# Gating expert rows in their slot and adding them to a DRAM copy of x

## The reference, cut to what matters

```python
# x: (8, 256, 256) float32 = 2048 tokens of 256 numbers = 8 images of 256 x 256
h = layernorm(x); h = instance_norm(h over the tokens of an image) * gamma[id] + beta[id]
gates, idx = top_k(softmax(h @ router_w), 2); gates /= gates.sum(-1)     # 2 of 8 experts per token
hid  = relu(einsum('nd,edf->nef', h, exp_w1) + exp_b1)                   # 256 -> 1024
eout = einsum('nef,efd->ned', hid, exp_w2) + exp_b2                      # 1024 -> 256
f = x + sum over the token's 2 experts of gate * eout                    # the field
df = -(d/dx (A0 f) + d/dy (A1 f)) + 0.5 * (d2/dx2 (B0 f) + d2/dy2 (B1 f) + 2 mixed terms of B2 f)
out = maximum(f + df * dt[image], 0)
```

## Time and profile before

| | us |
|---|---|
| median of 3 runs (lowest to highest) | 358.14 (357.94 to 358.56) |
| the profiled execution: its own time | 359.56 |
| its span, first to last instruction | 357.7 |

### The profile page before, as it was taken

The page is one execution under the profiler, slowest core; times in us unless marked ns, Lnnn a source line. Parts: engine busy times, 40 slices in busy tenths (PEclk is TensorE's granted clock), DMA queues, the critical chain, the costliest instruction groups (busy, mean ns, idle before and its releaser), DMA issues.

```text
span 357.7 us, 6562 instructions
## 1 busy us (share of the span) xinstructions
PE 304.5 (85%) x1963; PEld 265.1 (74%) x1963; DVE 285.9 (80%) x523; ACT 252.5 (71%) x465; POOL 161.1 (45%) x135
## 2 busy tenths in 40 slices
PE   1759231999999999999999999999999988477896
PEld 0648231999999999999999999999999978132334
DVE  3896683678889889988988989988898893299991
ACT  1688214696998799699699979969988870188421
POOL 2565306333345545533533554453354413287650
PEclk9999755799999999999999999999999999699999
DMA  8903453976687877766768786776784500596822
GB/s 271 379 4 112 125 196 119 381 250 217 202 263 265 287 251 236 270 225 223 281 217 275 264 278 205 239 256 220 226 274 158 158 3 30 160 309 118 179 100 79
DMA packets 49860, 74.27 MB, mean 208 GB/s; under 512 B 3349, under 2 KB 40751, under 8 KB 49712
## 3 DMA queue, kind: packets, MB, share of 16 engines
q1 hardware_dynamic: 45104, 62.29, 53.4%
q0 software_dynamic: 4368, 11.54, 10.5%
q10 hardware_dynamic: 368, 0.20, 0.2%
HBM read 63.51 MB, written 9.31 MB: 204 GB/s over the span
## 4 chain that ended last, share of the span: by engine, by line
PE 71%; DVE 12%; DMA 8%; ACT 3%; issue 3%; POOL 1%; SPq 1%; DVEq 0%; POOLq 0%; ACTq 0%
PE psum L1005 23%; PE psum L1032 19%; PE psum L1034 10%; PE psum L998 5%; PE psum L974 2%; PE psum L1000 2%; DMA raw_b<-in_L_cond_exp_w_dram 2%; PE psum L1027 2%; DMA t_y<-y_rows 1%; PE psum L1069 1%; PE psum L913 1%; PE psum L924 1%; DMA x_sb<-t_y 1%; DMA gathered<-h_rows,src_cur 1%; DMA x_sb<-in_x_dram 1%
## 5 line engine op out<-in xcount | busy, mean ns | idle before, releaser
L798 POOL DMA_INDIRECT gathered<-h_rows,src_cur x40 | 65.4, 1635 | 123.3 <-DVE src_cur L1336 95.6
L1032 PE MATMUL psum<-w_split,hid 128*128 128x512 f32 x296 | 106.6, 402 | 1.4 <-DVE y_sb L1388 1.4
L1005 PE MATMUL psum<-slot_h,w_split 128*128 128x256 f32 x768 | 97.3, 287 | 2.1 <-DVE slot_h L1353 2.1
L1005 PEld LDWEIGHTS psum<-slot_h,w_split 128*128 128x128 f32 x768 | 95.4, 194 | 3.3 <-issue 2.7
L1034 PE MATMUL psum<-w_split,hid 128*128 128x256 f32 x296 | 83.0, 280 | 0.0
L1347 DVE TENSOR_TENSOR w_split<-raw_b,w_split 128x2048 fp32r<-128x2048 f32 x23 | 52.7, 2292 | 20.4 <-ACT w_split L621 20.4
L1032 PEld LDWEIGHTS psum<-w_split,hid 128*128 128x128 f32 x296 | 55.6, 188 | 13.8 <-issue 1.6
L653 ACT ACTIVATE hid<-relu 128x512 fp32r<-128x512 f32 (+1 forms) x92 | 51.0, 591 | 15.8 <-DVE relu L1359 15.8
L811 POOL DMA_INDIRECT y_rows<-y_sb,dst_cur x39 | 48.7, 1248 | 28.6 <-issue 11.6
L644 ACT ACTIVATE relu<-psum,b_cur 128x256 f32<-128x256 f32 x128 | 53.6, 489 | 6.1 <-PE psum L1005 4.3
L1341 DVE TENSOR_TENSOR w_split<-raw_a,w_split 128x2048 fp32r<-128x2048 f32 x23 | 52.6, 2285 | 4.8 <-DMA gathered<-h_rows,src_cur 2.9
(11 more groups left out here) (183 smaller groups left out, 391.9 us busy)
## 6 DMA issues: line engine op xcount, KB each, us to landing
raw_a<-in_L_cond_exp_w_dram SPq DMA_DIRECT2D x23, 1024.0 KB, 6.2
raw_b<-in_L_cond_exp_w_dram SPq DMA_DIRECT2D x23, 1024.0 KB, 5.6
t_y<-y_rows SPq DMA_DIRECT2D x6, 512.0 KB, 8.5
x_sb<-in_x_dram SPq DMA_DIRECT2D x4, 512.0 KB, 6.6
h_rows<-h_tok SPq DMA_DIRECT2D x16, 128.0 KB, 2.2
x_sb<-t_y POOLq DMA_DIRECT2D x4, 512.0 KB, 4.7
out_dram<-t_out SPq DMA_DIRECT2D x3, 512.0 KB, 3.0
b_all<-in_L_cond_exp_b_dram SPq DMA_DIRECT2D x1, 1024.0 KB, 10.1
```

What stands on the lines that cost most here:

```text
L798: pool.indirect_dma_start(out=gathered[:, par, t, :], out_offset=None, in_=h_rows, in_offset=bass.IndirectOffsetOnAxis(ap=src_cur[:, par, ...
L1005: last = pe.matmul(banks[bank][:, ST * (blk % 2):ST * (blk % 2) + rows], w_split[:, 0, par, w, at:at + P], slot_h[:, par, h, k, 0:rows], s ...
L1032: pe.matmul(out.rearrange("p (w d) -> p w d", w=2), hid[:, par, 0, blk, P * t:P * t + P], w_split[:, 1, par, :, D * blk:D * blk + D], star ...
```

## The change

`y_rows` is gone. A new DRAM tensor `f_rows` starts as a copy of x (row 0 a filler, 2048 token rows, and 256 spare rows for the empty places of singles and pairs), written by SP from `x_sb` in five DMAs after the rows of h. A small DRAM tensor `g_rows` holds the 4096 gates: PE transposes `gates`, ACT copies them out of PSUM and stores them. Per slot, POOL gathers the gates by one more indirect DMA per 128 rows (4 bytes per row), DVE multiplies each 128 rows of `y_sb` by their gates (semaphore `y_gated`), and the scatter adds into `f_rows` (`compute_op=ALU.add`) where before it wrote into `y_rows`. Since the two rows of a token come from different slots, each scatter first waits until the scatter of the slot ahead has landed. In the last slot DVE gates the bias ahead of time (`b2_last`) and folds the gate into the instruction that reads PSUM. The stencil loads `f_rows` straight into `x_sb` (2 MB where before 4 MB), and `add_up`, `gated`, `plus`, `add_y1` and `add_y2` are gone.

```diff
@@ SP, after the stores of h_rows
+            for i in range(4):
+                sp.wait_ge(x_in[i], 16)
+                sp.dma_start(f_rows_tok[:, 4 * i:4 * i + 4, :], x_sb[:, 4 * i:4 * i + 4, :]).then_inc(f_init, 16)
+            sp.dma_start(f_rows[1 + N:1 + N + TB * P, :].rearrange("(t p) d -> p t d", p=P),
+                         x_sb[:, 0:TB, :]).then_inc(f_init, 16)
             sp.wait_ge(e_ok, 1)
@@ SP, after the last slot
             for i in range(2):
-                for c, buf in enumerate((Y1, Y2)):
-                    sp.dma_start(buf[0][:, 2 * D * i:2 * D * i + 2 * D].rearrange("p (j d) -> p j d", j=2),
-                                 y_rows_tok[c, :, 2 * i:2 * i + 2, :]).then_inc(y_first[c][i], 16)
+                sp.dma_start(x_sb[:, 2 * i:2 * i + 2, :], f_rows_tok[:, 2 * i:2 * i + 2, :]).then_inc(f_first[i], 16)
             for g in range(1, NPAIR):
-                for c, buf in enumerate((Y1, Y2)):
-                    sp.dma_start(buf[g].rearrange("p (j d) -> p j d", j=4),
-                                 y_rows_tok[c, :, 4 * g:4 * g + 4, :]).then_inc(y_in[c][g], 16)
+                sp.dma_start(x_sb[:, 4 * g:4 * g + 4, :], f_rows_tok[:, 4 * g:4 * g + 4, :]).then_inc(f_in[g], 16)
@@ ACT, after the router's exponentials
+            act.wait_ge(gates_turned, 1)
+            act.activation(gate_t[:, :], banks[5][0:TOPK * NJ, 0:P], ACT.Copy).then_inc(gates_left, 1)
+            act.wait_ge(gates_left, 1)
+            load(g_rows[1:1 + TOPK * N, :].rearrange("(r p) d -> r (p d)", p=P), gate_t[:, :], gates_out)
@@ ACT, stencil (gated() is gone)
             keep(0)
+            keep(1)
             for g in range(NPAIR):
...
                 for i in range(2):
-                    if g == 0 and i == 0:
-                        act.wait_ge(t_first, 1)
...
+                    if g == 0:
+                        act.wait_ge(f_first[i], 16)
                     else:
-                        act.wait_ge(y2_added[g], 16)
+                        act.wait_ge(f_in[g], 16)
@@ POOL
+            def gather_gates(k, m):
+                par = k % 2
+                for t in range(width(k)):
+                    pool.indirect_dma_start(
+                        out=gate_cur[:, k % TURNS, t:t + 1], out_offset=None, in_=g_rows,
+                        in_offset=bass.IndirectOffsetOnAxis(ap=idx_cur[:, par, t, 1:2], axis=0),
+                    ).then_inc(gate_in[par], 16)
             def scatter(k, m, halves=False):
                 s, par = at_slot(k, m), k % 2
-                pool.wait_ge(y_half if halves else y_ok, 1 if halves else s + 1)
+                pool.wait_ge(y_half if halves else y_gated, 1 if halves else s + 1)
                 pool.wait_ge(dst_ok, s + 1)
+                if k >= 1:
+                    pool.wait_ge(y_out[1 - par], moved(k - 1, m))
...
-                        out=y_rows, out_offset=bass.IndirectOffsetOnAxis(ap=dst_cur[:, par, t:t + 1], axis=0),
-                        in_=y_sb[:, par, t, :], in_offset=None, bounds_check=TOPK * N - 1, oob_is_err=False,
+                        out=f_rows, out_offset=bass.IndirectOffsetOnAxis(ap=dst_cur[:, par, t:t + 1], axis=0),
+                        in_=y_sb[:, par, t, :], in_offset=None, compute_op=ALU.add,
                     ).then_inc(y_out[par], 16)
+            gather(0, None)
+            pool.sem_inc(first_sent, 1)
+            gather(1, None)
+            pool.wait_ge(gates_out, 32)
+            pool.wait_ge(gate_idx_ok, 1)
+            gather_gates(0, None)
+            gather_gates(1, None)
...
             with pool.Fori(1, ROUNDS + 1) as m:
                 for k in range(FIRST, FIRST + TURNS):
                     gather(k + 2, m)
+                    gather_gates(k + 2, m)
                     scatter(k - 2, m)
@@ PE, after the ranks; and at the head of the stencil
+            pe.wait_ge(gates_ok, 1)
+            pe.transpose(banks[5][0:TOPK * NJ, 0:P], gates[:, :, :].rearrange("p c j -> p (c j)"),
+                         ident).then_inc(gates_turned, 1)
-            pe.wait_ge(y_first[0][0], 16)
+            pe.wait_ge(y_gated, NS)
             for par in range(2):
+                if par == 1:
+                    pe.wait_ge(f_first[0], 16)
@@ DVE, source(k) and finish(k)
                 dve.wait_ge(rows_in[par], moved(k - 2, m))
+                dve.wait_ge(gate_in[par], moved(k - 2, m))
-                dve.tensor_copy(src_cur[:, par, 0:w], src_i[:, bass.DynSlice(at, w)]).then_inc(src_ok, 1)
+                dve.tensor_copy(idx_cur[:, par, 0:w, :], idx_i[:, bass.DynSlice(at, w), :]).then_inc(src_ok, 1)
...
                 right(0, w).then_inc(y_ok, 1)
+                dve.wait_ge(gate_in[par], moved(k, m))
+                dve.wait_ge(y_ok, s + 1)
+                for t in range(w):
+                    last = dve.tensor_scalar(y_sb[:, par, t, :], y_sb[:, par, t, :], gate_cur[:, k % TURNS, t:t + 1],
+                                             None, ALU.mult)
+                last.then_inc(y_gated, 1)
```

More of the change, by code:

```diff
@@ L357, in moe_then_stencil @@
         next_in = [sem(f"next_in{par}") for par in range(2)]
[L358 to L361, removed]
+        t_keep, t_fd = sem("t_keep"), sem("t_fd")
         t_gf_pool, t_s_pool = sem("t_gf_pool"), sem("t_s_pool")
@@ L378, in field, with field_in @@
         def field(g):
-            return FV[0] if g == 0 else x_sb[:, 4 * g:4 * g + 4, :].rearrange("p j d -> p (j d)")
-        TURNS = 6
+            return x_sb[:, 4 * g:4 * g + 4, :].rearrange("p j d -> p (j d)")
+        def field_in(engine, g):
+            if g > 0:
+                engine.wait_ge(f_in[g], 16)
+            else:
+                engine.wait_ge(f_first[0], 16)
+                engine.wait_ge(f_first[1], 16)
         FIRST, ROUNDS = 4, 3
@@ L520, in _ @@
             sp.wait_ge(hrows_out, 16 * (NJ + 1))
+            sp.wait_ge(f_init, 16 * 5)
+            sp.wait_ge(gates_out, 32)
         @block.scalar
@@ L704, in _ @@
             act.wait_ge(l2_done, NS)
-            act.wait_ge(y_ok, NS)
+            act.wait_ge(y_gated, NS)
             def keep(g):
@@ L1391, in finish @@
                 if halves:
-                    for t, (done, out) in enumerate(((l2_half, y_half), (l2_done, y_ok))):
+                    dve.wait_ge(gate_in[par], moved(k, m))
+                    for t in range(w):
+                        dve.tensor_scalar(b2_last[:, t, :], bias.rearrange("p e d -> p (e d)"),
+                                          gate_cur[:, k % TURNS, t:t + 1], None, ALU.mult).then_inc(b2_gated, 1)
+                    dve.wait_ge(b2_gated, w)
+                    for t, (done, out) in enumerate(((l2_half, y_half), (l2_done, y_gated))):
                         dve.wait_ge(done, 1 if t == 0 else s + 1)
-                        dve.tensor_tensor(y_sb[:, par, t:t + 1, :],
-                                          banks[LAST_BANKS[t]][:, 0:D].rearrange("p (t d) -> p t d", t=1),
-                                          bias, ALU.add).then_inc(out, 1)
+                        dve.scalar_tensor_tensor(out=y_sb[:, par, t, :], in0=banks[LAST_BANKS[t]][:, 0:D],
+                                                 scalar=gate_cur[:, k % TURNS, t:t + 1], in1=b2_last[:, t, :],
+                                                 op0=ALU.mult, op1=ALU.add).then_inc(out, 1)
                     return
@@ L1477, in edge_cols @@
                 return ends[:, :, 0:D // 4:D // 4 - 1, :]
-            def add_up():
-                for i in range(2):
-                    for c, y, dst in ((0, Y1, F0), (1, Y2, FV)):
-                        dve.wait_ge(y_first[c][i], 16)
-                        for j in range(2 * i, 2 * i + 2):
-                            at = slice(D * j, D * j + D)
-                            last = dve.scalar_tensor_tensor(
-                                out=dst[0][:, at], in0=y[0][:, at], scalar=gates[:, c, j:j + 1],
-                                in1=x_sb[:, j, :] if c == 0 else F0[0][:, at], op0=ALU.mult, op1=ALU.add)
-                        if c == 0:
-                            link(last)
-                    if i == 0:
-                        last.then_inc(t_first, 1)
-                last.then_inc(t_f, 1)
             def wide(v):
```

105 lines of the change are left out of this document (44 added, 61 removed).

## The result

The changed kernel takes 371.05 us (median of 4 runs, 369.98 to 371.85), the kernel before 358.04: a ratio of 1.0368, 95% interval 1.0349 to 1.0388. It is slower, where the forecast was 356.8. The profiled execution of the changed kernel took 369.98 us, its span 368.2.

What follows compares the result with a forecast made beforehand. PE was taken to bound the slots and DVE the stencil. Stencil -1.7, DVE +0.2, POOL 0 and front +0.2 summed to -1.3 us, from a median of 358.14 to 356.8 us; range 354.2 to 362.0.

Steps and rivals of the forecast that it cites:

- The slots, POOL: POOL's queue in the slots: 39 more indirect DMAs fit within each round of three slots, so 0 us.
- barely: POOL in the slots: fifteen DMAs with stretching take 27.2 of a round's 30.29 us, so POOL just keeps up.
- The third rival: POOL's queue in the slots: slower once the average unstretched DMA exceeds 1.18 us; +10, 366.8 us; chance 0.14 with other late waits.
- The slots, DVE: DVE's gating in the slots: 0.34 us per multiplication, nearly all hidden ahead of layer 1; entered as +0.2 us.
- 1.26 of 1.33 us: DVE ahead of `low_h`: two pairs' gating adds 1.26 us against 1.33 of slack before PE's layer 1, so free.
- The stencil: After the slots: saved loads and `add_up` pay for serial scatters; pair 1 gains 1.50, pair 2 0.17; -1.7 us.
- The front: Before the slots: extra stores and gate gathers against a less stretched first gather; bounds -1.5 and +2.0, entered +0.2 us.
- The sum: Whole kernel: -1.7 + 0.2 + 0 + 0.2 = -1.3 us, giving 356.8 us.
- what would show it wrong: Signs: PE waiting for `gathered` or `slot_h`; POOL without idle time in a round; a scatter landing in over 4 us undisturbed.

Runs made afterwards that it cites:

- e4: Changed kernel, but odd slots' scatters add into a second DRAM copy of x and no scatter waits for the slot ahead: 359.98 us.
- e3c: Changed kernel with plain scatters and without gate gathers, DVE still multiplying, by a tile of ones: 357.79 us.
- e9: Changed kernel with plain scatters, gate gathers kept, and a filling POOL instruction (iota of 128 x 170) behind each scatter: 361.11 us.
- f2: Changed kernel with gates put in order by PE instead of gathered by POOL, and DVE's gating moved to the end of its step: 374.76 us.
- e6: Changed kernel with plain scatters, no gate gathers and no DVE gating in slots 0 to 21: 355.82 us, ratio 0.9923 to the kernel before.
- e1: Changed kernel, but its scatters write instead of adding: 358.40 us, ratio 1.0021 to the kernel before.
- the four corners: Changed kernel's slots: plain scatters without gate gathers 219.54 us, plain with 219.80, adding without 219.72, adding with 228.67.
- e8: Changed kernel without gate gathers, SP sending as many 4-byte packets by direct DMA instead: 363.01 us.
- e7: Changed kernel with each gate gather replaced by a POOL iota of about its length that sends no packets: 370.28 us.

## Why the prediction was wrong, point by point

**The slots, POOL: forecast 0, measured 9.1 us (all but the gating and 0.5).** This is the step that failed, at two places. The first is a price: an adding scatter was taken to occupy POOL for 0.97 us as a plain one; undisturbed it takes 1.56. In the prediction's own sum that makes 27.2 + 5 x 0.59 = 30.15 of 30.29 us: "barely" became nothing, and e4 shows just this queue, 60.0 of 60 us. The second is the sentence that the scatter's new wait is for a transfer issued a slot, 10 us, earlier. In the queue without slack POOL came to the wait at 165.60 - 1.45 = 164.15, 4.8 us after it had issued the transfer (159.40 above), and landings take a median of 5.5 and up to 8.8 us. The wait found its transfer still under way, 10.3 us in six waits, five of 1.3 to 1.5 in the slots and the last, 3.1, in the stencil. What this did to PE is read from the windows of the slots, of the changed kernel and of e3c:

```profile
84.94:313.61 228.67, 219.53 (x1552) 204.98 (x1550) 200.91 (x309) 179.66 (x328) 180.89 (x102) 0.99 0.74 214
```
```profile
86.58:306.12 219.54, 216.91 (x1552) 202.22 (x1550) 200.72 (x309) 180.13 (x328) 95.66 (x69) 1.00 0.67 223
```

Of the 9.1 us between them, (228.67 - 219.53) - (219.54 - 216.91) = 6.5 are idle time of PE, 5.6 of it in three waits for `gathered`. The other 2.6 are the same 1552 matmuls taking longer; the two stretches at a granted clock of 0.83 and 0.85 fit that. The prediction had no term for that. A term of 0 stood on a cover, and the cover was the slack that another term of the same sum used up.

**The third rival** (POOL's queue, 0.14, 366.8 us) named the right place but a condition that did not decide. Its threshold was an average unstretched DMA of 1.18 us; the rows give (5 x 1.56 + 5 x 0.97 + 5 x 0.95) / 15 = 1.16. The queue stayed just below, and without the wait it would have kept up, as in e4. With the gating in place the loss needs the wait and the late landing besides (e4, e9), and it comes with a queue that has room too, if the data is late (f2).

**The slots, DVE: forecast +0.2, measured +1.6 (e3c less e6).** The price was right for a gating instruction that nothing disturbs: 0.35 us, and 0.62 for a pair's two, against 0.34 and 0.26 + 0.34 = 0.60. What was wrong is the sum of what piles up ahead of `low_h`, 1.26 of 1.33 us: a margin of 0.07 is none. In six rounds of e3c the two pairs' gating takes some 0.72 and 0.77. One of them:

```profile
189.68 0.77 DVE L1405 TENSOR_SCALAR y_sb<-y_sb,ones 128x256 f32<-128x256 f32 x2
```

With these lengths the prediction's sum is 1.26 + 0.12 + 0.17 = 1.55, more than the 1.33 of cover (an estimate from these rows), and the rows of e3c under e6 show the cover gone. What lengthens the gating no run tried: a gather of POOL runs beside each of these, but one runs beside a pair's gating of 0.62 us too (97.77 us).

**The stencil: forecast -1.7, measured +0.4.** The chain has the steps that the prediction gave it; the rows of the changed kernel's POOL:

```profile
310.43 1.56 POOL L830 DMA_INDIRECT f_rows<-y_sb,dst_cur  x1 [6.03 <-DVE dst_cur L1392]
312.29 1.56 POOL L830 DMA_INDIRECT f_rows<-y_sb,dst_cur  x1 [0.30 <-issue]
316.96 1.56 POOL L830 DMA_INDIRECT f_rows<-y_sb,dst_cur  x1 [3.12 <-DMA f_rows<-y_sb,dst_cur]
318.82 1.56 POOL L830 DMA_INDIRECT f_rows<-y_sb,dst_cur  x1 [0.30 <-issue]
```

and, from the chain that ended last:

```profile
318.82 3.67 DMA f_rows<-y_sb,dst_cur
```

The last rows land 322.49 - 313.61 = 8.9 us after the last `y_sb`; the prediction had 309.97 - 303.47 = 6.5. The 2.4 between them are twice 0.59 for POOL's time and twice some 0.6 for the landing, taken at 3.1 and measured at 3.67. Both were mis-sized, the second within its bounds. What follows came as forecast: 4.70 us to DVE's second instruction (4.78), 7.90 from there to pair 1 (8.03), since line 1549, the old line 1541, takes 1.14 to 1.21 instead of 2.56, and 8.41 to pair 2 (8.56):

```profile
327.19 0.69 DVE L1532 TENSOR_TENSOR psum<-gr,psum 128x508 f32<-128x508 f32 x1 [0.61 <-ACT psum L752]
332.69 1.21 DVE L1549 TENSOR_TENSOR t_d1b2f<-t_b2f 128x1016 f32<-128x1016 f32 x1
335.09 1.21 DVE L1532 TENSOR_TENSOR psum<-gr,psum 128x1016 f32<-128x1016 f32 x1
...
343.50 1.21 DVE L1532 TENSOR_TENSOR psum<-gr,psum 128x1016 f32<-128x1016 f32 x1
```

With plain scatters the stencil gains 4.0 us (e1), with adding ones that don't wait 2.8 (e4): the serial, adding tail eats all that the short loads bring.

**The front: forecast +0.2, measured -1.1**, within its bounds of -1.5 and +2.0; in the other runs it lies between -2.0 (f2) and +2.4 (e9).

**The sum.** By the spans: front -1.1, slots 0.5 + 1.6 + 9.1, stencil +0.4: +10.5. The 0.5, between the kernel before and e6, no run explains. Of what would show it wrong, the prediction had named PE waiting for `gathered` and POOL without idle time in a round; both came.

## What to carry to other kernels

Before a wait is costed at nothing because its transfer was sent long ago, add up the queue that the wait stands in with the new instructions at their upper bounds: a queue without slack moves issue and wait together, and what waits behind, here the gathers, pays. An in-order engine that sends both the last step of one slot and the first step of a later one should not wait for the first in front of the second. And where two changes are each covered alone, run them together and apart: the four corners here differ by 0.3 us and by 9.

## What the runs showed of the hardware that was not expected

- An indirect DMA of 128 rows of 1 KB that adds in DRAM occupies POOL for 1.56 us, against 0.97 for one that writes (e1), and takes 3.67 us from start to landing with little else under way, against 2.10 before. In the slots the medians were 5.5 and 4.2 (e1; 4.7 in the kernel before).
- An indirect gather of 128 rows of 4 bytes occupies POOL for 0.95 us, as long as one of 128 rows of 1 KB (0.97): the bytes of a row do not set it. As many packets of 4 bytes sent by SP cost the kernel nothing (e8).
- A multiplication by a per-partition scalar on DVE, 128x256, SBUF to SBUF, is held up by a POOL instruction that only writes: two took 1.71 us beside an iota of 0.84 (e7), 0.62 alone.
